# Attention kernel: scores follow the max products by eleven slots, not twelve

## Time and profile before

| What | Value |
|---|---|
| Time, median of 3 runs | 997.32 us (995.33 to 997.86) |
| Time of the profiled execution | 996.6 us |
| Span of its trace | 994.8 us |
| TensorE busy | 926.4 us, 93% |
| VectorE busy | 799.7 us, 80% |
| ScalarE busy | 617.3 us, 62% |
| GpSimd busy | 353.3 us, 36% |
| Mean granted TensorE clock | 0.965 |

### The profile page before, as it was taken

How to read it: one execution, slowest core, us unless ns; L and a number is a source line. 1 busy time by engine, 2 the same in 40 slices (tenths; PEclk the granted TensorE clock), 3 DMA queues, 4 the chain that set the end, 5 groups by cost and what they waited for, 6 DMA issues and landing times.

```text
span 994.8 us, 16452 instructions
## 1 busy us (share of the span) xinstructions
PE 926.4 (93%) x6178; PEld 373.3 (38%) x6180; DVE 799.7 (80%) x1566; ACT 617.3 (62%) x720; POOL 353.3 (36%) x472
## 2 busy tenths in 40 slices
PE   5879999999999999999999999999999989947985
PEld 3323332323343344333343343332423423136763
DVE  4687879898979878889889879889799798074765
ACT  3116778777867777877767777777677678801110
POOL 3052002004734253129643623257243232922113
PEclk9778999999999999999999999999999999977998
DMA  5924120620260305201631033104430001150001
GB/s 135 154 33 62 47 54 12 100 58 8 75 110 23 95 13 83 69 13 39 104 102 60 10 56 81 31 7 105 91 96 12 12 14 55 60 180 22 0 1 64
DMA packets 60613, 58.33 MB, mean 59 GB/s; under 512 B 19141, under 2 KB 49621, under 8 KB 60149
## 3 DMA queue, kind: packets, MB, share of 16 engines
q1 hardware_dynamic: 59844, 55.96, 25.5%
q0 software_dynamic: 384, 1.05, 0.3%
q10 hardware_dynamic: 304, 0.26, 0.2%
HBM read 18.00 MB, written 9.17 MB: 27 GB/s over the span
## 4 chain that ended last, share of the span: by engine, by line
PE 78%; DVE 9%; ACT 4%; issue 3%; DMA 2%; POOL 2%; SPq 1%; ACTq 0%; POOLq 0%; DVEq 0%
PE obank L1053 22%; PE sc L1039 19%; PE ring L1020 15%; PE ring L936 9%; PE ring L943 4%; DVE mx L1288 4%; PE sc L1131 3%; ACT prob L855 2%; PE ring L928 2%; DVE st L1206 2%; DMA x_sb<-x 1%; PE sc L943 1%; DMA qp<-parts 1%; PE ring L1063 1%; ACT zT L758 0%
## 5 line engine op out<-in xcount | busy, mean ns | idle before, releaser
L1288 DVE TENSOR_REDUCE mx<-ring 128x1 f32<-128x512 f32 x1024 | 634.5, 682 | 107.8 <-PE ring L1020 106.7
L855 ACT ACTIVATE prob<-sc 128x1024 f32<-128x1024 f32 x512 | 496.0, 1022 | 131.7 <-PE sc L1039 130.5
L1039 PE MATMUL sc<-qp,kp 48*128 48x512 bf16 (+1 forms) x2048 | 275.2, 380 | 1.7 <-ACT prob L855 1.1
L1053 PE MATMUL obank<-prob,vaug 128*32 128x512 f32 x2048 | 273.6, 606 | 0.7 <-ACT prob L855 0.7
L1020 PE MATMUL ring<-kp,qp 48*128 48x512 bf16 x1024 | 246.3, 392 | 16.9 <-DVE mx L1288 12.8
L1020 PEld LDWEIGHTS ring<-kp,qp 48*128 48x128 bf16 x1024 | 75.0, 93 | 296.3 <-DVE mx L1288 228.3
L1039 PEld LDWEIGHTS sc<-qp,kp 48*128 48x128 bf16 (+1 forms) x2048 | 98.9, 95 | 106.3 <-ACT prob L855 24.7
L614 POOL TENSOR_TENSOR hid<-hid,b 128x512 f32<-128x512 f32 x24 | 30.3, 1272 | 110.6 <-ACT hid L816 110.6
L1053 PEld LDWEIGHTS obank<-prob,vaug 128*32 128x32 f32 x2048 | 40.3, 108 | 66.1 <-issue 64.2
L628 POOL TENSOR_TENSOR resid<-qkf,parts 128x1024 f32<-128x1024 f32 x11 | 23.5, 2137 | 115.7 <-ACT parts L792 115.7
L622 POOL TENSOR_TENSOR yA<-yA,sums 128x512 f32<-128x512 f32 x15 | 19.1, 1273 | 111.2 <-DMA sums<-reciprocal_scratch 111.2
(11 more groups left out here) (197 smaller groups left out, 781.9 us busy)
## 6 DMA issues: line engine op xcount, KB each, us to landing
kp<-parts SPq DMA_DIRECT2D x96, 128.0 KB, 4.9
qp<-parts SPq DMA_DIRECT2D x189, 64.0 KB, 2.7
x_sb<-x SPq DMA_DIRECT2D x7, 1024.0 KB, 6.3
out<-hid SPq DMA_DIRECT2D x4, 1024.0 KB, 5.1
yA<-oT SPq DMA_DIRECT2D x126, 32.0 KB
sums<-reciprocal_scratch SPq DMA_DIRECT2D x31, 128.0 KB
x_scratch<-x SPq DMA_DIRECT2D x3, 1024.0 KB, 4.5
qp<-mp SPq DMA_DIRECT2D x128, 2.0 KB
```

Source lines behind the costliest of these rows:

```text
L855: nc.scalar.activation(prob[:, e % 2, 2 * a:2 * a + 2, :].rearrange("p g n -> p (g n)"), sbuf2[a][:, :], ACT.Exp, scale=0.25).then_inc(s_f ...
L1039: ins = nc.tensor.matmul(dst[:, j * HALF:(j + 1) * HALF], kp[rows, h, kt * P:(kt + 1) * P], qp[rows, qh, h, :], start=plane == 0, stop=pla ...
L1053: ins = nc.tensor.matmul(obank[i * VW:(i + 1) * VW, :], vaug[:, b % 2, kt, c0:c0 + VW], prob[:, v % 2, i, :], start=(kt == 0), stop=(kt == ...
L1288: nc.vector.tensor_reduce(mx[:, u % 2, n:n + 1], src[:, :], AX.X, ALU.max).then_inc(rv_free, 1)
```

## The change

`LEAD` goes from 12 to 11, and the four entries of `D_AT` go down by one. Nothing else is edited, but three things hang on LEAD: the scores and value products of every unit come one slot earlier against its max products, the copies of the results, the store and the load on SP and the reciprocals on VectorE come one slot earlier, and the loop has one slot fewer (270 in place of 271). `MT_AT`, the fill tables and the pack steps stay where they were. Between the slot of a unit's transpose and the slot of its first scores there are two slots in place of three (one in place of two for the units that end a batch). Within SP's queue the load `reciprocals_in` of a unit, which stood in the same slot as a transpose and behind its four transfers, now stands one slot ahead of them.

```diff
-LEAD = 12
+LEAD = 11
 SLOTS = NS + LEAD + 3
...
-D_AT = (43, 51, 14, 19)
+D_AT = (42, 50, 13, 18)
```

## The result

| | Time, us | Ratio to the kernel before |
|---|---|---|
| before, 4 runs | 996.33 median (993.05 to 997.86) | |
| changed, 4 runs | 1005.27 median (1004.13 to 1006.43) | 1.0099, 95% interval 1.0076 to 1.0121 |

The account below looks back on a forecast made before the run. The prediction took TensorE and VectorE to bound the kernel together. Its terms for head, late units, projection and tail summed to +2.3 us, giving 998.9 against the profiled execution and 999.6 against the median, range 997.0 to 1003.5.

Parts of the forecast that it names:

- Rival 1: SP's wait for the store delays the maxima at units 9, 17 and 25: +7.3 us, 1004.6; chance 17%.
- Two signs: Would show it wrong: waits at units 9 and 17; last max product over 4 us or under 0.5 behind its old time.
- Unit 6, +1.7: First batch, tau 57: SP late amid its packs, so scores wait for the maxima, +1.7 us, bounds +0.8 and +1.9.
- Unit 25, +1.4: Last batch, tau 17: load waits for its store on SP, delaying the maxima; wait 0.7 to 1.5, taken as +1.4 us.
- Units 9 and 17, +0.1: Same tau as unit 25 in earlier batches, same order with more room: together +0.1 us, bounds 0 and +2.
- Projection, -0.9: Tau 21 of the last batch: TensorE's 0.93 us idle for POOL's product goes as the load is issued earlier, -0.9.
- Head, +0.1: Unit 0: full clock returns one slot earlier, as the engine fills one slot earlier; +0.1 us, kept -0.4 to +1.4.
- rival 2: At the head, the clock comes back at its old time: +1.3 us on the sum, 1000.9; chance 13%.
- Tail, -0.1: Unit 31: the slot removed at the end becomes a wait of 2.6 us for its maxima; -0.1.
- The sum: Over the whole kernel: +0.1 + 1.7 + 1.4 + 0.1 - 0.9 - 0.1 = +2.3 us.
- The rule of the Trainium skill: Store ahead of unit 25: fixed DMA cost of about 2.0 us would mean no wait there, sum 1.4 lower; set aside.

Follow-up runs that it names:

- Run 1: Changed kernel with 14 to 16 extra matmuls ahead of the wait for the maxima at units 6, 17 and 25; ratio 1.0050 to the kernel before.
- run 5: Kernel before (LEAD 12) with only SP's copies, store and load, VectorE's reciprocals and `D_AT` one slot earlier; ratio 1.0068, median 1002.01 us.
- run 4: Changed kernel with the pack steps of batches 1 to 3 at tau 16 to 27 in place of 12 to 23; ratio 1.0031.
- run 2: Changed kernel with the load of the reciprocals one slot later, behind the four transfers of the maxima; ratio 1.0014, median 997.05 us.
- run 6: Kernel before with LEAD 11 for TensorE and ScalarE only; SP's steps, reciprocals and `D_AT` at their old slots; ratio 1.0000, median 995.98 us.
- run 3: Changed kernel with only the loads of units 7, 15 and 23 one slot later, behind the maxima's transfers; ratio 1.0044.
- repaired kernels: Changed kernel, load behind the maxima's transfers, next batch's packs and batch-ending transpose earlier: 0.9997; second form, transpose earlier only for last unit, wait behind half its scores: 0.9987.
- run 8: The two repaired kernels, both edited from the changed kernel; ratios 0.9997 for the first form and 0.9987 for the second.
- run 9: The kernel before, unedited, executed once more for a second profile; 995.3 us, span 993.4.

## Why the prediction was wrong

Point by point, by the steps of the prediction:

- **The mechanism and the places** were right in the main: TensorE waits for the maxima at units 6, 25 and 31, the load stands ahead of the transfers on SP, and SP stands still for the store. Rival 1, all three late units and 1004.6, was the nearest case in time; it had 17%. It was not right as told: unit 9 doesn't wait, and unit 25 idled 1.94, not 3. Two signs that the prediction had named for being wrong came: a wait at unit 17, and the last max product 7.7 us behind its old time.
- **Unit 6, +1.7.** The wait measured 1.71. The step failed in what stands behind it: the slot lost 3.06. The prediction said that what is lost in front of the scores is lost, and never asked what the gap does to TensorE's clock, though the head of the same kernel showed it at half clock after idling. Run 1 shows that this is the cause, and the two waits of run 5 show it again. It is the step that failed: the costs of units 6, 17 and 25 were each mis-sized by a term of about 1.4 to 1.7 us. The wait itself came out as forecast with the long issue among the packs (2.97) that the prediction counted on; in run 4's trace it was not met, and the wait was 0.56, under the lower bound of 0.8.
- **Unit 25, +1.4.** The wait is 1.94. The store took 6.4 to land, not the 5.4 that the sum used; 6.8 stood in the earlier trace rows and was kept for the rival. The recorded sum has a slip of 0.2 at its upper end (697.3 + 0.6 + 1.9 is 699.8, not 700.0), and the 6.8 was met at unit 9 and not at this place; neither decides anything. With the clock the slot lost 3.67.
- **Units 9 and 17, +0.1.** Unit 9: none, as said. Unit 17 waited 2.08, just above the bound of 2 that was given for both. Its room was taken to be larger by the earlier issue in the trace of before, but once SP stands still for the landed store, what SP did earlier no longer counts; its slot runs 495.96 to 501.20, 2.75 lost, and the slot behind it is slow as well. This was the second failure.
- **Projection, -0.9.** The wait is gone in the changed kernel. But the second trace of before has 0.46 at that place in place of 0.93, and runs 2 and 6 show none either, though their load doesn't stand ahead of the maxima. So the term was worth 0.5 to 0.9 against the traces of before, and that the load's new place brought it isn't shown.
- **Head, +0.1.** Right as told: the scores of slots 11 to 13 start at the distances of the old ones (68.02 to 76.03 is 8.01 again), and the clock came back at 76.72, so rival 2 did not come. From the first max pair of slot 11 to the scores of slot 15 it is 13.45 (67.81 to 81.26) where it was 13.61 (70.88 to 84.49): -0.2 in place of +0.1.
- **Tail, -0.1.** Right: 28.2 us from the last max pair to the last value product in the changed kernel (848.80 to 877.03) and in before (841.09 to 869.31). The wait is 2.62 where 2.6 was said. That the clock can fall behind this wait too was missed. It did in the traces of runs 1, 2, 3, 4 and 6, which all wait 2.6 there, and not in the changed kernel's.
- **The sum.** 3.06 + 2.75 + 3.67 = 9.5 in the three slots, some 1 more in the slot behind unit 17, less 0.5 to 0.9 for the projection: about 10, where the medians lie 8.9 apart. The forecast had 3.2 for these places. Of what is missing some 5 us are the clock (1.4, 1.7 and 1.7 with the slot behind unit 17), 2 the wait of unit 17 and 0.5 the longer wait of unit 25. Single spans bear this out only roughly. Against the second trace of before (993.4) the span grew by 9.1, but that trace has a fall of the clock at 721.90 which the changed kernel's lacks. Against the first (994.8) it grew by 7.7, but that one came 3.0 later to slot 11 and lacks the fall at tau 49.
- **The rule of the Trainium skill** (DMA: Bandwidth & Descriptors, the two cost components under the anatomy of one DMA, a fixed cost of about 2.0 us) was rightly set aside for a store behind 128 KB copies: 6.4 us. Where no other packets move, in run 4, the store took 1.4 us, also less than the rule says. On that page of the Trainium skill the figure is fitted to transfers issued by GpSimd, while these are issued by SP.

Why the repaired kernels aren't faster than before is not settled. The slot at the end is 2.2 us shorter and the projection's wait was expected to go. Small waits came (0.52 at unit 5, 0.38 at unit 31), the end of the program took 1.4 longer than in the second trace of before, and falls of the clock behind gaps of 1.1 to 1.3 us in the last batch come in some executions (runs 5, 8 and 9), which hides differences of this size. How often they come in each kernel was not measured.

## What to carry to other kernels

Before a transfer is moved in an in-order queue, list what now stands behind it and what it waits for, and price the wait with the landing time under the traffic at that place, not with the median of its kind. Where two engines bound each other with no slack, price a new gap of some 2 us on TensorE between its own length (2.3 lost for 2.24 in run 5) and nearly twice that (3.67 for 1.94), since the clock may fall behind it; if the gap can't be removed, matmuls into a buffer that is overwritten anyway can hold the clock. Split a change that edits one constant into the orders it touches: here the lead alone was free (1.0000), the order alone cost 0.7%, and 0.3% came only from both together. Take a second profile of the same kernel before a stretch is called free of something: the first one here was the only one of twelve without a fall at tau 49.

## What the runs showed of the hardware that was not expected

A gap of 1.71 us on TensorE among otherwise full slots was followed by a stretch at 1.2 GHz (213.30 to 216.70, clock 0.51), and so were gaps of 1.58 (run 3), 1.94 and 2.08; gaps of 0.55 and 0.56 (runs 2, 4 and 6) were not. The length of the gap doesn't settle it: one of 2.24 left the clock at 1.00 (run 5), one of 1.14 did not (run 9), one of 2.6 before unit 31 was followed by a fall in five of six traces, and one of 2.7 at tau 49 in eleven of twelve. What else decides is open. An 8 KB store needed 1.4 us to land with no other packets moving, and 5.4, 6.4 and 6.8 behind packs of 128 KB.
